# The last expert layer adds weighted rows into a sum in DRAM, and three changes that come with it

## The reference

```python
def _L1_ffn_ref(x, gate_w, w1, w2, w3):          # H, F, E, K = 512, 800, 8, 2
    logits = xt @ gate_w.T
    probs = jax.nn.softmax(logits, axis=-1)
    top_vals, top_idx = jax.lax.top_k(probs, K)
    top_vals = top_vals / jnp.sum(top_vals, axis=-1, keepdims=True)
    w_full = jnp.zeros((T, E), dtype=xt.dtype).at[jnp.arange(T)[:, None], top_idx].add(top_vals)
    h1 = jnp.einsum('th,efh->tef', xt, w1)
    h3 = jnp.einsum('th,efh->tef', xt, w3)
    act = jax.nn.silu(h1) * h3
    expert_out = jnp.einsum('tef,ehf->teh', act, w2)
    y = jnp.einsum('te,teh->th', w_full, expert_out)
...
x = x + 0.5 * _L0_ffn_ref(_layernorm(x, axis=-1), ...)
x = x + _L0_attn_ref(_layernorm(x, axis=-1), ...)
x = x + 0.5 * _L0_ffn_ref(_layernorm(x, axis=-1), ...)
x = x + 0.5 * _L1_ffn_ref(_layernorm(x, axis=-1), ...)
x = x + _L1_attn_ref(_layernorm(x, axis=-1), ...)
x = x + 0.5 * _L1_ffn_ref(_layernorm(x, axis=-1), ...)
```

## Time and profile before

| what | value |
|---|---|
| median of 3 runs | 1252.48 us (1247.73 to 1256.41) |
| profiled execution, its time | 1256.9 us |
| its span | 1255.1 us |
| PE busy | 1170.2 us, 93% of the span |
| DVE busy | 866.6 us, 69% |
| ACT busy | 352.6 us, 28% |
| POOL busy | 138.6 us, 11% |
| mean granted clock of PE | 0.959 of full speed |

### The profile page before, as it was taken

The page is one execution under the profiler, slowest core; times in us unless marked ns, Lnnn a source line. Parts: engine busy times, 40 slices in busy tenths (PEclk is TensorE's granted clock), DMA queues, the critical chain, the costliest instruction groups (busy, mean ns, idle before and its releaser), DMA issues.

```text
span 1255.1 us, 28179 instructions
## 1 busy us (share of the span) xinstructions
PE 1170.2 (93%) x9962; PEld 527.7 (42%) x9962; DVE 866.6 (69%) x2483; ACT 352.6 (28%) x746; POOL 138.6 (11%) x191
## 2 busy tenths in 40 slices
PE   6899988999999999899899999999979899999992
PEld 3467663443333333344344444444624333333330
DVE  4731575977777785578889999932558578777753
ACT  5433621001010101332166777783110010101010
POOL 2200021001010101344000000000110010101010
PEclk9889978999999999999999999999789999999996
DMA  9100415147832535517604333007731645616566
GB/s 359 55 1 1 155 69 189 36 146 274 288 119 64 194 124 184 202 54 179 173 3 86 52 58 46 2 2 280 295 147 39 241 165 191 218 35 221 166 207 235
DMA packets 63668, 174.33 MB, mean 139 GB/s; under 512 B 9885, under 2 KB 16627, under 8 KB 61351
## 3 DMA queue, kind: packets, MB, share of 16 engines
q1 hardware_dynamic: 55471, 150.60, 37.2%
q0 software_dynamic: 5760, 18.88, 4.3%
q10 hardware_dynamic: 2296, 3.05, 0.7%
HBM read 785.47 MB, written 22.03 MB: 643 GB/s over the span
## 4 chain that ended last, share of the span: by engine, by line
PE 80%; DVE 8%; DMA 5%; issue 2%; ACT 2%; SPq 2%; POOL 0%; ACTq 0%; POOLq 0%; DVEq 0%
PE PS L1108 30%; PE PS L1127 14%; PE PS L1633 6%; PE PS L1620 5%; PE PS L1598 5%; PE PS L822 3%; PE PS L806 3%; PE PS L1660 2%; PE PS L1548 2%; PE PS L586 2%; DVE PS L1756 2%; PE PS L1553 1%; PE PS L570 1%; PE PS L1623 1%; DMA arena<-y_scratch 1%
## 5 line engine op out<-in xcount | busy, mean ns | idle before, releaser
L1108 PE MATMUL PS<-arena 128*32 128x400 f32 x3456 | 400.1, 505 | 9.2 <-DMA HH<-in_w 5.3
L1108 PE MATMUL PS<-HH,arena 128*32 128x400 f32 x1152 | 399.4, 505 | 0.0
L1108 PEld LDWEIGHTS PS<-arena 128*32 128x32 f32 x3456 | 148.0, 111 | 250.2 <-issue 241.7
L1298 DVE STREAM_TRANSPOSE arena<-arena 32x192 f32<-32x192 f32 x576 | 211.4, 367 | 7.2
L1127 PE MATMUL PS<-arena 128*32 128x512 f32 x1512 | 194.1, 596 | 4.0 <-DVE arena L1298 4.0
L1756 DVE CUSTOM_DVE_ANT_0 PS<-PS,U 128x128 f32<-128x128 f32 (+7 forms) x256 | 186.7, 786 | 15.6 <-PE PS L1598 15.2
L1276 DVE STREAM_TRANSPOSE arena<-arena 32x128 f32<-32x128 f32 x544 | 164.6, 303 | 15.8 <-DMA arena<-h_scratch,RT 7.8
L1703 ACT ACTIVATE arena<-PS 128x512 f32<-128x512 f32 (+3 forms) x384 | 160.1, 513 | 54.9 <-PE PS L1623 48.3
L1181 ACT ACTIVATE arena<-PS 128x400 f32<-128x400 f32 x72 | 36.2, 503 | 427.4 <-PE PS L1108 427.2
L1282 DVE TENSOR_TENSOR arena<-arena,PS 128x400 f32<-128x400 f32 x72 | 41.0, 572 | 132.7 <-ACT arena L1181 132.6
L1108 PEld LDWEIGHTS PS<-HH,arena 128*32 128x32 f32 x1152 | 126.6, 111 | 0.0
(11 more groups left out here) (259 smaller groups left out, 1268.8 us busy)
## 6 DMA issues: line engine op xcount, KB each, us to landing
arena<-in_w SPq DMA_DIRECT2D x456, 800.0 KB
arena<-in_w2a SPq DMA_DIRECT2D x266, 768.0 KB
HH<-in_w SPq DMA_DIRECT2D x152, 800.0 KB
HH<-in_w2a SPq DMA_DIRECT2D x38, 768.0 KB
arena<-split_scratch SPq DMA_DIRECT2D x96, 128.0 KB, 6.2
arena<-y_scratch SPq DMA_DIRECT2D x24, 256.0 KB, 5.5
split_scratch<-arena SPq DMA_DIRECT2D x8, 768.0 KB, 4.6
arena<-in_wqkv SPq DMA_DIRECT2D x3, 1024.0 KB, 6.9
```

The costliest lines, as they stand in the source:

```text
L1108: mm = eng.matmul(PS[SR * j:SR * j + SR, 2 * hf + m, 0:FH], XBT[:, u, c, SR * j:SR * j + SR], W13[j][:, c // 2, m, c % 2, hf * FH:(hf + 1) ...
L1298: tr = eng.transpose(ACT_T[SR * b:SR * b + SR, u, :, rows], src[:, :, SR * b:SR * b + SR])
```

## The change

In the last layer (f = 1):

- DVE works out three index lists and the index of each row's weight; SP writes the weights `WT` to `weight_scratch`, and POOL gathers them with 18 indirect DMAs of 128 numbers, so that ACT can scale a result by its weight while it copies it out of PSUM (into parts of X, `Y2`, in place of `YB`).
- SP writes X to `sum_scratch` (1024 rows), and 512 further rows of any finite content, to which padding and rows of the other pass go.
- Each group of four results (steps 0 to 15) is scattered twice, with an addition in DRAM: once for the pairs that are a row's first choice, and after a wait for all four again for the second choices (`sum_rows`).
- When all of these have landed, SP copies the sum to the output, DRAM to DRAM, and POOL gathers the 256 rows of steps 16 and 17 from the sum (`SOFAR`). PE multiplies the two results with matrices that say which rows have the same token (`SAME`, from two small matmuls and three comparisons), DVE adds, and two scatters write the rows to the output, the first after the copy, the second after the first. The reload, the additions on DVE and the eight stores are gone.

In both layers:

- The down loads and tails are issued by ACT (`act_down_in`), which reads the experts itself; SP issues the up loads alone.
- In the last step DVE transposes the first three chunks only; PE transposes the other three within down(16) (`turn_last`), ACT copies them (`m_atl`).

In the first layer SP waits for PE at the end in another way (`m_w2`, `m_y`), ahead of the same loads for attention.

Of the diff, the core:

```diff
+        def experts(eng, p):
+            found = []
+            for j in range(NSTR):
+                q = j * NSTEP + p
+                x = eng.value_load(EBX[q:q + 1, 0:1], min_val=0, max_val=2 * NE - 1)
+                found.append((bass.ds(x % NE, 1), x >= NE))
+            return found
+
+        def act_down_in(eng, f, p, now):
+            for half in range(2):
+                if p == 0:
+                    eng.wait_ge(w2_in[half], N2 * (LOADS * f + 1))
+                else:
+                    eng.wait_ge(S(("m_w2f", "m_w2")[half]), NSTEP * f + p)
+                for j in range(NSTR):
+                    down_in(eng, j, half, *now[j])
+            if p >= QUAD:
+                eng.wait_ge(S("m_y"), NSTEP * f + y_done(p - QUAD))
+            for j in range(NSTR):
+                tail_in(eng, p, j, now[j][0])
...
+                if f == 1 and p == 0:
+                    eng.wait_ge(S("s_wt"), 1)
+                    eng.dma_start(WD.rearrange("(i p j) o -> p i (j o)", p=P, j=TOPK), WT).then_inc(S("s_hd"), 16)
+                if f == 1 and p == 2:
+                    eng.wait_ge(S("s_hd"), HD_DONE + 16)
+                    for i in range(NT):
+                        eng.dma_start(AS[i * P:(i + 1) * P, :], X[:, i, :]).then_inc(S("s_hd"), 16)
+                    for j in range(QUAD):
+                        eng.dma_start(AS[T + j * P:T + (j + 1) * P, :], X[:, j, :]).then_inc(S("s_hd"), 16)
+            if f == 1:
+                eng.wait_ge(y_out[1], Y_BEFORE + 16 * GROUPED)
+                eng.dma_start(out[:, :], AS[0:T, :]).then_inc(S("s_out"), 16)
+                return
...
+            def sum_rows(first):
+                if first == 0:
+                    eng.wait_ge(S("s_hd"), AS_DONE)
+                else:
+                    eng.wait_ge(y_out[1], Y_BEFORE + 16 * first)
+                for q in range(first, first + QUAD):
+                    eng.wait_ge(S("m_yc"), NSTEP * f + q + 1)
+                    eng.indirect_dma_start(AS[:, :], bass.IndirectOffsetOnAxis(ap=SUM0[:, q:q + 1], axis=0),
+                                           Y2[q], None, compute_op=ALU.add).then_inc(y_out[0], 16)
+                eng.wait_ge(y_out[0], Y_BEFORE + 16 * (first + QUAD))
+                for q in range(first, first + QUAD):
+                    eng.indirect_dma_start(AS[:, :], bass.IndirectOffsetOnAxis(ap=SUM1[:, q:q + 1], axis=0),
+                                           Y2[q], None, compute_op=ALU.add).then_inc(y_out[1], 16)
...
+                for j in range(2):
+                    p = NSTEP - 2 + j
+                    eng.wait_ge(s_x, NT * (k + 1) + j + 1)
+                    if j == 0:
+                        eng.wait_ge(S("s_out"), 16)
+                    else:
+                        eng.wait_ge(y_out[0], Y_BEFORE + 16 * (GROUPED + 1))
+                    eng.indirect_dma_start(out[:, :], bass.IndirectOffsetOnAxis(ap=GIDX[:, p:p + 1], axis=0),
+                                           SOFAR[j], None).then_inc(y_out[j], 16)
...
+            def turn_last(f):
+                eng.wait_ge(S("m_act"), 2 * NSTEP * (f + 1))
+                eng.wait_ge(S("m_yc"), NSTEP * (f + 1) - 3)
+                for c in range(FC // 2, FC):
+                    tr = eng.transpose(PS[:, 6, (c - FC // 2) * P:(c - FC // 2 + 1) * P], AC[:, c * P:(c + 1) * P], ident[:])
+                tr.then_inc(S("m_last"), 1)
...
-                    eng.copy(YB[:, u, :], PS[:, y_bank(q), :]).then_inc(S("m_yc"), 1)
-            if f == 1:
-                for u in range(2):
-                    eng.wait_ge(y_out[u], 8 * NSTEP * (f + 1))
-                for i in range(NT):
-                    rows_back(eng, i, 1)
```

More of the change, by code:

```diff
@@ L981, in sp_moe @@
             eng.wait_ge(S("s_eb"), f + 1)
[L982 to L985, removed]
-                    for j in range(NSTR):
[L987 to L1012, removed]
-                    if q >= QUAD:
-                        eng.wait_ge(S("m_y"), NSTEP * f + y_done(q - QUAD))
-                    for j in range(NSTR):
-                        tail_in(eng, q, j, late[j][0])
-                late = now
@@ new lines, in sp_moe @@
+            for p in range(NSTEP):
+                now = experts(eng, p)
+                for c in range(C):
+                    if p == 0:
+                        eng.wait_ge(w13_in[c], N13 * (LOADS * f + 1))
+                    else:
+                        done = NSTEP * f + p - 1
+                        if c < C - 1:
+                            eng.wait_ge(S("m_wf"), (C - 1) * done + c + 1)
+                        else:
+                            eng.wait_ge(S("m_h"), 2 * done + 2)
+                    for j in range(NSTR):
+                        up_in(eng, j, c, *now[j])
+                if f == 1 and p == 0:
[7 more added lines that the diff above has]
+                        eng.dma_start(AS[T + j * P:T + (j + 1) * P, :], X[:, j, :]).then_inc(S("s_hd"), 16)
@@ L1121, in down @@
                     eng.wait_ge(S("m_yc"), NSTEP * f + max(p - QUAD + 1, 0))
+                if f == 1 and p == GROUPED - 3:
+                    eng.wait_ge(S("s_diag"), 2)
+                    for j in range(2):
+                        mm = eng.matmul(PS[:, 7, j * P:(j + 1) * P], ones[:], OWN[j], start=True, stop=True)
+                    mm.then_inc(S("s_tokens"), 1)
+                if f == 1 and p == GROUPED - 1:
+                    eng.wait_ge(S("s_pairs"), 1)
                 for c in range(FC):
@@ L1149, in pe_moe @@
             down(NSTEP - 1)
+            if f == 1:
+                eng.wait_ge(S("m_yc"), NSTEP * (f + 1))
+                eng.matmul(PS[:, 6, :], SAME[NSTEP - 1, NSTEP - 1], Y2[NSTEP - 1], start=False, stop=True,
+                           skip_group_check=True).then_inc(S("s_sum"), 1)
             if f == 0:
@@ L1172, in act_moe @@
             eng.copy(XBT[:, 0], PS[:, 6, :].rearrange("p (c t) -> p c t", c=C)).then_inc(S("m_xfirst"), 1)
+            eng.wait_ge(S("s_eb"), f + 1)
+            now = experts(eng, 0)
+            act_down_in(eng, f, 0, now)
+            now = experts(eng, 1)
             for p in range(NSTEP + 1):
@@ L1265, in dve_moe @@
             link(eng.tensor_scalar(WT[:, :, 0], DEN, 0.5, None, ALU.mult))
-            link(eng.tensor_tensor(WT[:, :, 1], WT[:, :, 0], LESS, ALU.mult))
+            weights = eng.tensor_tensor(WT[:, :, 1], WT[:, :, 0], LESS, ALU.mult)
+            if f == 0:
+                link(weights)
+            else:
+                weights.then_inc(S("s_wt"), 1)
             def turn_rows(p):
@@ L1798, in _ @@
                     sp_attn1(sp, k)
-            for i in range(NT):
-                sp.wait_ge(s_x, NT * len(SL) + i + 1)
-                sp.dma_start(out[i * P:(i + 1) * P, :], X[:, i, :]).then_inc(S("s_out"), 16)
-            sp.wait_ge(S("s_out"), 16 * NT)
+            sp.wait_ge(S("s_out"), 16)
+            for u in range(2):
+                sp.wait_ge(y_out[u], Y_BEFORE + 16 * (GROUPED + 1))
         @block.gpsimd
```

115 lines of the change are left out of this document (104 added, 11 removed).

## The result

The changed kernel takes 1255.56 us in the median of 22 runs (1247.94 to 1260.98), the kernel before 1250.56 of 22 (1246.43 to 1256.41): ratio 1.0040, interval 1.0026 to 1.0055. So it is slower by 0.4%, 5 us, which is small but clear of no change, where I had forecast 17 us less. The two profiles alone say something else: the changed kernel's span is 1250.4 us, 4.7 less than the 1255.1 of the earlier trace rows. The profiled execution of the kernel before was a long one (1256.9 against a median of 1250.6), that of the changed kernel a short one (1252.2 against 1255.6). A second profile of the kernel before is among the experiments.

What follows compares the result with a forecast made beforehand. TensorE's back-to-back up and down products bound both expert layers, with 23.5 us after them. End -13.1, queue -3.4, last step -1.5, layer start +0.3, small things +0.4 gave -17.3 us: 1235 us, range 1226 to 1250.

Steps and rivals of the forecast that it cites:

- the price of a group of adding scatters: Last layer's end: each group of four scatters takes 1.5 us longer for adding in DRAM than a plain group.
- As much again: Upper bound on what additions cost a group of four scatters: 6.6 us, the time a plain group takes.
- slow accumulation: Rival, chance 0.09: additions slow each group, kernel slower than before from 10.2 us a group; at 18 us, 1268 us.
- expensive copy and additions: Rival, chance 0.24: additions at +5 us a group and the copy at 15 us leave -4.3 us, 1248 us.
- That is the end: Last layer: the kernel ends at 1242.0 when the second output scatter lands, with no reload, sums or stores after; -13.1 us.
- The base: The profiled execution of the kernel before, 1256.9 us for a span of 1255.1, used for the sum and scaled to 1252.48.
- Down weights from ScalarE's queue: Last layer's expert change at step 4: SyncE issues up loads 3.35 us sooner without the down loads; -3.4 us.
- fall into 950 to 959 ... and SyncE waits: Last layer's start: SyncE's 3 MB of writes for the sum's start, 8 us of traffic, come when no weights move.
- Last step: Step 17 of both layers: sharing transposes between VectorE and TensorE starts down(17) earlier; -1.5 us in the first layer.
- covered: ScalarE's loads, tails and value loads, 6.3 us after a down product, fit before the next silu some 9 us after it.
- The weights' gathers: Last layer's start: 18 small gathers at 1.30 us each, 23.4 us, ahead of step 3's row gather; cost 0.
- The copy, 9: Last layer's end: SyncE's DRAM-to-DRAM copy of 2 MB to the output takes 9 us, ending at 1236.0.

Runs made afterwards that it cites:

- plain: The changed kernel with plain scatters into the sum in place of adding ones, so the output is not the sum: 0.9974 of the kernel before.
- nodrain: The changed kernel without GpSimd's drain at the end of the last stage: 1.0021 of the kernel before.
- the three with mended ends: The changed kernel without the stage's drain (1.0021), with attention weights behind the first layer's tails (1.0038), or with both and step 17's first-half loads before ScalarE's copy (1.0054).
- halfadds: The changed kernel with the second choices' scatters plain and the first choices' still adding: 0.9986 of the kernel before.
- again: The kernel before, unchanged, run once more for a second profile: ratio 1.0014, span 1246.5 us.
- nocopy: The changed kernel with the copy of the sum to the output cut to its first 128 rows: 0.9995 of the kernel before.
- sumonly: The changed kernel without the queue split and TensorE's share of the last transposes, the sum in DRAM kept: 1.0102 of the kernel before.

## Why the prediction was wrong, point by point

*The step that failed: the price of a group of adding scatters, "so I take the low side, 1.5 per group".* The end's two groups were given 16.5 us, 13.5 for plain scatters and 3.0 for the additions; they took 23.2. Two things are in the 6.7 us. The additions cost 5.9 (23.2 against 17.3 in plain), not 3.0: I argued from bytes, 1 MB read twice and written once, and the bytes were not the limit. POOL needs 1.57 us for one in place of 0.97, and the engines 1.15 us more each. The other 3.8 are there without any addition, nearly all in the second group, 10.4 us in plain: the sum priced it as if nothing else moved, while step 17's down loads were on the engines. That they are the cause is read from the timeline; no run takes them away. "As much again", the bound that I had named (6.6), holds for the end's groups; in two earlier groups the four first choices cost 6.5 and 7.1 us more than in plain, and one of them went over the 15 us that I had named as the sign of being wrong (15.4).

The rival *slow accumulation* had the mechanism and the sign, but by its own price (from 10.2 us a group on) it should not have come. The size, +5 a group, stood in *expensive copy and additions*. That this rival's -4.3 us is close to the -4.7 between the two profiles is luck: the copy took 8.6 us, not 15, and the drain, which no rival named, has its place.

*"That is the end."* It was not: 4.7 us lie between the last landing and the program's end, GpSimd's drain. I read the end of the kernel before, where the drain is hidden, and did not ask what had to follow a POOL transfer that is last. nodrain shows that leaving out the stage's own drain does not take it away.

From down(15)'s end the end was forecast 38.5 us later and came after 51.4: +0.4 to the first scatter, +6.7 the groups, +0.8 the gather under the copy with the sum behind it, +0.3 the two scatters, +4.7 the drain. Down(15) itself ended at 1198.96, where the forecast puts it (1203.5 less 4.6). So against its own profile nearly the whole miss of 12.6 us is at the end. That the first part came out right is luck in part: the first layer gave nothing, up(0) ran 1.5 us shorter, up(4) and the step before it gave 5.0 instead of 3.4, 1.7 of it the first profile's clock, and steps 14 to 16 lost 2.4 to the new matmuls and to up(15)'s wait.

*The base.* I made the sum against one long execution, whose two clock drops and late start of up(0) were in it, and trusted that the changed kernel would share them. Between profiles the forecast of -17.3 became -4.7; between medians it is +5.0. The 9.7 us between these are how far the two profiled executions lay from their medians, 6.3 above and 3.4 below. The kernel before has 304.3 us of products in its second profile where the sum used 308.9; the changed kernel and the three with mended ends have 307.7 to 312.5. The additions' part in this is shown for step 15 (plain, halfadds). Most of the rest is behind up(17): from its start to the last tail it is 25.4 us in `again`, 27.9 in plain and 30.1 to 31.9 in the changed kernel, its mended forms, nocopy and halfadds, with a wait of 2.4 to 4.1 us ahead of or in down(17) and a granted clock of 0.50 for some 3 us in each of these six. In these kernels that stretch is not what the end waits for. Why the changed kernel's profiled execution was shorter than its median stays open.

*Down weights from ScalarE's queue, -3.4.* Right in the mechanism: 2.9 us at up(4), 1.1 more at the step before. What I left out was its service to the sum, up to 7.7 us. I had written that the writes "fall into 950 to 959 ... and SyncE waits"; sumonly shows that this holds only with the split.

*Last step, -1.5 in the first layer.* Failed in the whole kernel. VectorE's groups took 1.12 us (forecast 1.14) and down(17) of the first layer started 1.4 us earlier, but its tail waited 2.7 for weights that I had found "covered", and with that mended nothing is gained in the ratio. In the last layer the loads of step 17 arrive later than the transposes.

*The weights' gathers, 0.* Right: 18 of them 1.25 us apart, from 929.70 to 951.9, the row gather of step 3 at 952.17 (forecast 953.4). The rule of the Trainium skill (DMA: Bandwidth & Descriptors, Anatomy of one DMA) of 2.0 us each, laid end to end, would give an estimate of 36 us. The trace has 22.5 us, so most of the fixed part overlaps. The Trainium skill, in the same section, puts most of it into waiting for the write's receipt, and in this trace POOL does not wait for one between two gathers.

*The copy, 9.* It landed 8.6 us after its issue, where the formula of the Trainium skill, in the same section, gives an estimate of 6.8. What ended last was the gather beside it, by 0.4 us.

## What to carry to other kernels

A DMA that adds in DRAM is not a scatter with more bytes: price it by the time that POOL and the DMA engines are held. And price every transfer on the chain, plain ones too, beside the loads that run meanwhile: step 17's weights cost the end more than half as much as the additions did. All eight kernels here whose last transfer is a scatter of POOL end 7.15 to 7.45 us after that scatter starts, for a landing of 2.7; ask what has to follow the last transfer before it is moved to the end. Where an edit is worth 1%, take two profiles of the kernel before, or a stage's own length in them, before a sum is made against one.

## What the hardware showed that I had not expected

- An adding indirect DMA of 128 rows of 2 KB: 1.57 us on POOL against 0.97 for a plain one, 64 packets more, and 1.15 us more on the 16 DMA engines. Four of them and their landing take 11.6 to 15.4 us, by what moves beside them, against 6.9 to 8.4 for plain ones.
- GpSimd's drain behind a last scatter takes 7.14 us in every kernel with the sum (4.46 where that scatter was one of y_scratch), 4 us beyond its landing in the changed kernel, and a second drain pays it if the first is left out.
- A gather of 256 rows beside a DRAM-to-DRAM copy of 2 MB takes 8.8 us instead of about 4 beside one of 256 KB.
- The same program's start of the last layer varies by some 4 us between profiled executions, and in one of two a clock drop right behind a wait of TensorE added 1.7 us.
